# A graph network kernel: scatter one-hots of two layers read once for 13 of 25 tiles, those of the attention layer built during the propagation

## The reference

```python
h = relu(_layernorm(x)); x = x + propagate(h, src, dst)        # 10 iterations
#   msg = h[src] * norm[src];  agg = segment_sum(msg, dst)
#   h = 0.9 * agg * norm + 0.1 * h0
h = relu(_layernorm(x)); x = x + attention(h, rows=src, cols=dst, q, k, v)
#   att = exp(clip(q[rows] . k[cols])) per head, normalised over rows
#   out = segment_sum(att * v[cols], rows)
h = relu(_layernorm(x)); x = x + neighbours(h, edge_weight, ...)
#   segment_sum(h[src] * weight, dst) / deg, two 64x64 products
h = relu(_layernorm(x)); x = x + reviews(h * cj, ...) * ci
#   segment_sum(sigmoid(edge_attr @ ps_w) * h[src], dst)
```

## Time and profile before

| | |
|---|---|
| median of 3 runs | 1431.04 us (1430.93 to 1431.52) |
| profiled execution | 1421.67 us, its span 1420.0 us |
| TensorE matmuls busy | 1038.1 us (73%) |
| VectorE busy | 958.2 us (67%) |
| ScalarE busy | 566.7 us (40%) |
| GpSimd busy | 715.1 us (50%) |
| mean granted TensorE clock | 0.826 |
| DMA moved | 169.86 MB, mean 120 GB/s |

### The profile page before, as it was taken

One profiled execution on the slowest core, in us unless ns is written; L12 is line 12 of the kernel. 1 busy time (PEld: TensorE's weight loads), 2 busy tenths in 40 slices (PEclk: granted clock), 3 DMA queues, 4 the chain that ended last, 5 costly groups with the idle time before them and its releaser, 6 DMA issues.

```text
span 1420.0 us, 32164 instructions
## 1 busy us (share of the span) xinstructions
PE 1038.1 (73%) x12016; PEld 802.3 (57%) x12016; DVE 958.2 (67%) x1175; ACT 566.7 (40%) x1381; POOL 715.1 (50%) x444
## 2 busy tenths in 40 slices
PE   4956567877999999999934677767762766646764
PEld 3635457763555555555524677766662666545664
DVE  7885779993223223223255999999997788558875
ACT  1321127662010101101113766666651777417773
POOL 1000018888787878787888899999940000000000
PEclk9977655567999999999967878888765999759997
DMA  7642006551000000000012544444411889418894
GB/s 153 137 102 70 23 14 208 180 190 30 2 2 2 1 1 1 1 1 2 2 51 52 192 145 145 161 153 156 156 67 50 330 321 344 159 42 328 326 334 147
DMA packets 61492, 169.86 MB, mean 120 GB/s; under 512 B 32531, under 2 KB 33331, under 8 KB 61437
## 3 DMA queue, kind: packets, MB, share of 16 engines
q1 hardware_dynamic: 45371, 154.59, 30.5%
q10 hardware_dynamic: 2465, 13.60, 4.1%
q0 software_dynamic: 13600, 0.92, 3.5%
HBM read 144.28 MB, written 24.33 MB: 119 GB/s over the span
## 4 chain that ended last, share of the span: by engine, by line
PE 39%; DVE 31%; issue 15%; DMA 9%; ACT 3%; DVEq 2%; SPq 1%; ACTq 0%
PE ps L1424 24%; DMA hl_room<-slot_rows 7%; PE ps L1410 4%; DVE arena L809 3%; DVE base_room L804 3%; PE ps L1237 3%; PE ps L1298 2%; PE ps L1255 2%; DVE hl_room L998 2%; DMA hl_room<-in_edge_attr_dram 2%; DVE arena L886 2%; PE ps L1285 2%; DVE h_room L823 2%; DVE arena L823 1%; ACT arena L561 1%
## 5 line engine op out<-in xcount | busy, mean ns | idle before, releaser
L489 POOL DMA_INDIRECT w_table<-wpa,slot_i x425 | 710.4, 1672 | 329.3 <-ACT wpa L600 200.1
L1237 PE MATMUL ps<-arena 125*128 125x64 f16 (+1 forms) x3900 | 257.2, 218 | 165.7 <-ACT arena L528 75.6
L1424 PE MATMUL ps<-arena,hl_room 125*128 125x500 f16 (+1 forms) x1750 | 345.1, 353 | 9.1 <-DVEq L1062 9.1
L1237 PEld LDWEIGHTS ps<-arena 125*128 125x128 bf16 x3900 | 189.8, 105 | 181.8 <-ACT arena L528 74.6
L1424 PEld LDWEIGHTS ps<-arena,hl_room 125*128 125x128 f16 x1750 | 161.6, 100 | 169.7 <-issue 13.2
L1074 DVE TENSOR_TENSOR h_room<-ps,coef 125x256 f32<-125x256 f32 (+1 forms) x70 | 27.7, 396 | 271.5 <-PE ps L1410 271.5
L629 ACT ACTIVATE part_room<-ps 128x500 f32<-128x500 f32 (+1 forms) x70 | 38.0, 543 | 349.7 <-PE ps L1424 349.7
L1255 PE MATMUL ps<-arena 128*128 128x128 f16 (+1 forms) x1950 | 142.7, 238 | 21.6 <-DVE arena L818 9.8
L1242 PE MATMUL ps<-arena 125*128 (+1 forms) x1300 | 149.6, 214 | 0.0
L1255 PEld LDWEIGHTS ps<-arena 128*128 128x128 bf16 x1950 | 131.2, 108 | 24.3 <-issue 22.0
L791 DVE TENSOR_SCALAR arena<-hl_room,lane 125x3328 bf16<-125x3328 bf16 x100 | 108.3, 1086 | 48.8 <-DMA hl_room<-slot_rows 47.5
(11 more groups left out here) (244 smaller groups left out, 1336.1 us busy)
## 6 DMA issues: line engine op xcount, KB each, us to landing
hl_room<-slot_rows SPq DMA_DIRECT2D x100, 832.0 KB, 5.6
arena<-ohd_table SPq DMA_DIRECT2D x50, 832.0 KB, 5.8
hl_room<-in_edge_attr_dram ACTq DMA_DIRECT2D x17, 750.0 KB
w_table<-wpa,slot_i POOLq DMA_INDIRECT x425
ohd_table<-hl_room SPq DMA_DIRECT2D x13, 448.0 KB, 2.6
ohd_table<-base_room SPq DMA_DIRECT2D x12, 448.0 KB, 2.6
ohd_table<-hl_room SPq DMA_DIRECT2D x13, 384.0 KB
ohd_table<-base_room SPq DMA_DIRECT2D x12, 384.0 KB
```

The costliest lines, as they stand in the source:

```text
L489: pool.indirect_dma_start(w_table, bass.IndirectOffsetOnAxis(slot_i[:, u:u + 1], 0), wpa[:, u], None).then_inc(S[f"w_out{g % 2}"], 16)
L1237: last = pe.matmul(ps[:, m % RING, o:o + b - a], ohT[:, par, 0, k * L:(k + 1) * L], rhs, start=(i == 0), stop=(i == 1))
L1424: last = pe.matmul(ps[:, c, 0:w], hl[0:P, u, s, :], adj[:, s, c * CH * P:c * CH * P + w], start=(s == 0), stop=(s == T - 1))
```

## The change

1. **Layers 2 and 3:** the scatter one-hots of the even tiles (13 of 25) are loaded once, after the sums of the attention layer are taken, and stay in `kept_words` for both layers. Those of odd tiles are loaded in each layer into one room. TensorE waits for all kept loads before layer 2. The tables `parts2`, `ohT2` and `sums2` of these layers have places of their own.
2. **Attention layer:** VectorE no longer makes the scatter one-hots there. It makes them by halves during the propagation, after chunks 1 to 5 of each iteration, in the room of `xs`; SyncE writes each half to a table `ohs_table` in DRAM and loads a tile's one-hot (832 KB) in the layer. x is loaded again from the input after the last half is written, and VectorE waits for it before it goes on after the propagation.
3. **Propagation:** `part` is now a high and a low part in f16. ScalarE writes the high part scaled by 1/4096, VectorE the low part from PSUM and the high part; `combine` adds both with f16 matmuls, two per node tile, with 128 columns of weights instead of 125, and `coef` carries the factor. The bank of a chunk is free after VectorE's read.
4. **Edge weights:** the sigmoid is done in two parts: for 10 of 17 pieces of the features before the branch on the flag, for the other 7 in the old place. GpSimd starts its scatters after the first part and waits for the second before column 250. Its queue also issues the load of `wsl`, after the propagation.

```diff
                 def body(d, par, on, pair_no):
...
+                    if 2 in on and p == "l1":
+                        sp.wait_ge(S["l1_scat"], d - 1)
+                        sp.dma_start(ohd_words[:, par], ohs_table[bass.ds(d - 2, 1)].rearrange("t p x -> p (t x)")
+                                     ).then_inc(S[f"l1_ohd{par}"], 16)
+                    if 2 in on and p != "l1" and par:
                         sp.wait_ge(S[p + "_scat"], d - 1)
-                        sp.dma_start(ohd_words[:, par], ohd_table[bass.ds(d - 2, 1)].rearrange("t p x -> p (t x)")
-                                     ).then_inc(S[p + f"_ohd{par}"], 16)
+                        sp.dma_start(odd_words, ohd_table[bass.ds(d - 2, 1)].rearrange("t p x -> p (t x)")
+                                     ).then_inc(S[p + "_odd_oh"], 16)
...
+                with sp.Fori(0, T) as t:
+                    for half in range(2):
+                        a = sum(KG[:half]) * OW
+                        sp.wait_ge(S["ohs_made"], t * 2 + (half + 1))
+                        sp.dma_start(ohs_table[bass.ds(t, 1), :, a:a + KG[half] * OW].rearrange("t p x -> p (t x)"), ohs_words[half]
+                                     ).then_inc(S[f"ohs_out{half}"], 16)
+                for half in range(2):
+                    sp.wait_ge(S[f"ohs_out{half}"], 16 * (T + 1))
+                for a, b in SPLIT:
+                    sp.dma_start(xs[a:b, :, :], x.rearrange("(t p) f -> p t f", p=P)[a:b]).then_inc(S["x_back"], 16)
...
-                sp.wait_ge(S["w_placed"], 1)
-                sp.dma_start(wsl, w_table.rearrange("(r q) c -> r q c", r=L)).then_inc(S["wsl_in"], 16)
                 one_hots_kept(sp)
+                sp.wait_ge(S["l1_agg"], 1)
+                for k in range((T + 1) // 2):
+                    sp.dma_start(kept_words[:, k], ohd_table[2 * k]).then_inc(S["kept_in"], 16)
                 load_rows("l2", (0,))
...
                 for g in range(J // SU):
+                    if g * SU == EARLY * CJ:
+                        pool.wait_ge(S["pa_ready"], 2)
...
-                pool.sem_inc(S["w_placed"], 1)
+                pool.wait_ge(S["l0_done"], 1)
+                pool.dma_start(wsl, w_table.rearrange("(r q) c -> r q c", r=L)).then_inc(S["wsl_in"], 16)
...
             turned_features(0, EA_FLAG)
+            turned_logits(EARLY - 1)
+            act.wait_ge(S["z_back"], 1)
+            act.activation(wpa[:, 0:EARLY * CJ, 1], ps[0:P, 4, 0:EARLY * CJ], ACT.Sigmoid).then_inc(S["pa_ready"], 1)
...
-                            act.activation(part[:, n % 2, 0:w], ps[:, c, 0:w], ACT.Copy).then_inc(S["mains_taken"], 1)
+                            act.activation(part[:, n % 2, 0, 0:w], ps[:, c, 0:w], ACT.Copy, scale=1 / PSCALE).then_inc(S["part_high"], 1)
...
-                def ohd_of(s, par):
-
-                    vec.wait_ge(S[p + "_scat"], s - 1)
-                    vec.tensor_tensor(ohd[par], nodes(C), pairs(sls_h[:, bass.ds((s - 2) * C, C)], C),
-                                      ALU.is_equal).then_inc(S[p + "_ohd"], 1)
...
+                def low_sums(i, n):
+                    c = n % NCH
+                    w = min(CH, T - CH * c) * P
+                    vec.wait_ge(S["part_high"], i * (2 * NCH) + (n + 1))
+                    vec.scalar_tensor_tensor(part[:, n % 2, 1, 0:w], ps[:, c, 0:w], 1 / PSCALE, part[:, n % 2, 0, 0:w],
+                                             ALU.mult, ALU.subtract).then_inc(S["mains_taken"], 1)
...
+                def scatter_one_hots(t, k):
+                    j, half = k // 2, k % 2
+                    c, n = sum(KG[:half]), KG[half]
+                    vec.wait_ge(S[f"ohs_out{half}"], (t + j) * 16 + 16)
+                    vec.tensor_tensor(ohs_half[half], nodes(n), pairs(sls_h[:, bass.ds((t + j) * C + c, n)], n), ALU.is_equal
+                                      ).then_inc(S["ohs_made"], 1)
...
+                def two_iterations(i, more):
+                    for n in range(2 * NCH):
+                        u, c = n // NCH, n % NCH
+                        turn = c == NCH - 1
+                        if turn:
+                            new_nodes(i, n)
+                        if more or n + 1 < 2 * NCH:
+                            low_sums(i, n + 1)
+                        if not turn:
+                            new_nodes(i, n)
+                        if 1 <= c <= 5:
+                            scatter_one_hots(i * (T // (K0 // 2)), u * 5 + (c - 1))
...
                 vec.sem_inc(S["l0_done"], 1)
+                vec.wait_ge(S["x_back"], 32)
...
+                if p == "l2":
+                    pe.wait_ge(S["kept_in"], 16 * ((T + 1) // 2))
...
+                        if p == "l1":
+                            place = ohd[par][:, k // 2, :, k % 2]
+                        elif par:
+                            place = odd_oh[:, k // 2, :, k % 2]
+                        else:
+                            place = kept_oh[:, bass.ds(room, 1), k // 2, :, k % 2].rearrange("p k r -> p (k r)")
...
+            pe.wait_ge(S["z_turned"], EARLY)
+            for c in range(EARLY):
+                last = pe.transpose(ps[0:P, 4, c * CJ:(c + 1) * CJ], zT[0:CJ, c], ident[0:CJ, 0:CJ])
+            last.then_inc(S["z_back"], 1)
+            pe.wait_ge(S["pa_ready"], 1)
...
                     for k in range(min(CH, T - CH * c)):
-                        last = pe.matmul(ps[0:P, 7, k * D:(k + 1) * D], part[:, odd, k * P:(k + 1) * P], pair[:, :], start=True, stop=True)
+                        for e in range(2):
+                            last = pe.matmul(ps[:, 7, k * D:(k + 1) * D], part[:, odd, e, k * P:k * P + L], pair[:, :],
+                                             start=(e == 0), stop=(e == 1))
                     last.then_inc(S["combined"], 1)
```

149 lines of the change are left out of this document (85 added, 64 removed).

## The result

The changed kernel takes 1380.95 us (median of 4 runs, 1371.74 to 1385.22) beside 1431.28 for the kernel before in the same series: ratio 0.9634, 95% interval 0.9582 to 0.9685. The forecast was 1383, its range 1363 to 1408.

What follows compares the result with a forecast made beforehand. TensorE bounds the propagation, VectorE the attention layer, row loads layers 2 and 3. Terms -1.0 - 9.2 - 36 + 10 - 12 = -48.2 us take the profiled 1421.67 to 1373.5, median 1383; own range 1373 to 1394, wider 1363 to 1408.

Steps and rivals of the forecast that it cites:

- up to the propagation: Before the adjacency stage: transposes and a sigmoid moved early shorten VectorE's wait, 1.0 us off (0 to 1.5).
- propagation and reload, A to C: First multiplication of the propagation to the residual sum: combine gain less boundary waits, late end and reload, -9.2 us (-22 to +5).
- attention layer: Attention layer: tile period from 11.34 to 9.9 us, set by loads in SyncE's queue, 25 tiles: -36 us (-45 to -13).
- kept load, E to F: Attention sums to layer 2's first low part: 13 kept loads delay layer 2 by 10 us (6 to 14).
- layers 2 and 3: Layers 2 and 3: fewer one-hot loads, 4.8 us a tile, 6 us a layer, 12 us off in both (4 to 16).
- Combine: Propagation: f16 combine takes 0.27 us a chunk instead of 0.82, 32.8 us off in all (21 to 34).
- Boundary: Iteration ends in the propagation: TensorE waits 1.5 us for VectorE's updates, nine times, 13.5 us back (5 to 25).
- Rival (b): Propagation gives nothing back: each iteration boundary costs 3.5 us instead of 1.5, +18, time 1401; chance 0.14.
- Tail and reload: End of the propagation: last update ends later, +2.3 us, and VectorE waits for reloaded x, +7.8 (5 to 9).
- Rival (a): Attention layer held by loads: pair lands after 9 us, period 10.8, layer gives 13 us, time 1406; chance 0.17.
- (d): Slower through SyncE's queue: attention-layer loads land later than 11.0 us; at 12 us, period 12.3, time 1443; chance 0.04.
- Edge weights and the early sigmoid: GpSimd's scatters start about 110 us sooner, end near 950 to 990, before layer 2 wants the weights: hidden, 0.

Runs made afterwards that it cites:

- a1: The changed kernel once more, with no edit: 1373.66 us, ratio 0.9634 to the kernel before.
- c2: Changed kernel with VectorE building scatter one-hots in the attention layer again, none in the propagation, x not reloaded: 1380.64 us, ratio 0.9692.
- b2: a4 without the reload of x; the residual sum reads one-hots in its place, so part of the result is left out: 1366.68 us, ratio 0.9525.
- b4: a4 plus the edits of b1 and b3, and two kept tiles loaded ahead of the attention layer: 1361.68 us, ratio 0.9495.
- a4: Changed kernel with the attention layer's scatter one-hot loads issued by ScalarE instead of SyncE: 1359.35 us, ratio 0.9529.
- b3: a4 with the rows of layer 2's first two tiles loaded before the 13 kept loads, TensorE waiting at the first scatter: 1364.13 us, ratio 0.951.
- a2: Changed kernel with GpSimd's scatters starting only after the second sigmoid; early transposes and sigmoid stay: 1372.82 us, ratio 0.9624.
- a3: Changed kernel with the early part undone: all 17 transposes and one sigmoid behind the sort, GpSimd starting after them: 1377.61 us, ratio 0.9662.
- second series: Four edited kernels built on a4, b1 to b4, run on one chip beside the kernel before, whose median there was 1435.00 us.
- c4: a4 once more, with no edit, in the third series: 1359.74 us, ratio 0.9517.
- b1: a4 with the halves of scatter one-hots made in chunks 0 to 4 of each iteration instead of 1 to 5: 1365.49 us, ratio 0.9537.
- c1: a4 with VectorE's wait for the reloaded x moved behind the branch, directly ahead of the sum that needs it: 1356.39 us, ratio 0.9502.

## Why the prediction was right

Measured by a1 against the profile of before (the changed kernel's own profile in brackets), from the table. a1 is taken because its start of the propagation is that of the kernel before; the medians of the two series are 50.3 and 52.6 us apart.

| term | predicted | measured |
|---|---|---|
| up to the propagation | -1.0 | -0.6 (+10.1) |
| propagation and reload, A to C | -9.2 | -15.9 (-15.7) |
| C to D | 0 | +0.1 (-0.2) |
| attention layer | -36 | -26.2 (-25.7) |
| kept load, E to F | +10 | +7.1 (+6.9) |
| layers 2 and 3 | -12 | -13.5 (-11.9) |
| sum | -48.2 | -49.0 (-36.5) |

The mechanisms were right, stage by stage, but that the sum is right to 1 us is luck: an error of 10 us in the attention layer is cancelled by three of 1.5 to 6.7 on the other side.

**Combine.** 0.23 us instead of the 0.27 taken: 0.59 off a chunk, 35 us over the propagation by the prediction's own count (58 x 0.59 + 9 x 0.1). The nearest row, 33 ns a matmul, was the right one of the two; the measured 0.23 us is 29 ns each. (The other row gives 56 ns, 1.39 / 25, and not 59.)

**Boundary.** A to B fell by 27.0, so 8 of the 35 came back, not 13.5: 0.9 us an iteration instead of 1.5. c2 splits it: without the one-hots A to B falls by 32.6, so the one-hots cost 5.6 us, and 2.5 stay with the low sums and the shorter combine, which no run separates. The chain of VectorE's steps is the right mechanism, counted a little long: its last step ends 8.0 us after chunk 5's matmuls (449.5 to 457.5 in the timeline above), where 8.5 was worked out, and TensorE wants it at 7.7 (457.54 less the 0.35 of waiting), not 7.1. So the wait itself is a third of the 1.5, 0.48 us in the mean, less than the 1 to 2 us named as a sign. Most of the rest is in short waits of about 0.2 us ahead of the combine and of the next matmuls, 2.3 us in all, which c2 has too. Rival (b) is out.

**Tail and reload.** +10.1 predicted (2.3 and 7.8), +11.1 measured. Both transfers took longer than the sum had them: x is issued at 709.59 and awaited until 717.85, 8.3 us (6 taken), and in a1's chain the write takes 3.1 us (2.6 taken). So the wait was 10.72, but what the reload costs is 5.5 to 6.7 us (b2), since the gap behind the branch was shorter: 3.2 to 3.8 us in most kernels that wait there, 5.6 before and 5.95 in b2. That the wait shortens the gap is not shown: b4 has a wait of 9.5 and a gap of 6.0.

**Attention layer.** This is the term that was mis-sized most. The loop over SyncE's queue was named and a4 shows it: with the one-hots in another queue the period is 9.54, as VectorE alone would have it. But T was put at 9.9 for every tile; from the fifth pitch on it alternates between 9.55 and 10.8 or more, 10.15 in the mean of 24 pitches (766.6 to 1010.1 in a1). That is 6 of the 10 us. The loop closes over two tiles with the prediction's own three terms: the one-hot load is issued 6.06 us after the product (857.60 to 863.66), the rows are used 6.7 later (870.36), and the next but one product starts 7.74 after that (878.10), 20.5 us for two tiles. Two of the terms were right or long (7.74 and 7.06). The one that failed is the end of the scatter, put at 4.7 us with bounds of 3.4 to 5.3 (the row gives 3.5 for the lower): in the tile that sets the loop it is 6.06, in the other 3.93; why it ends so late there, no run isolates. The other 4 us are bookkeeping: I took 25 periods at 11.34, and the old layer has 24 pitches with a mean of 11.23 (782.4 to 1052.0) and a start and an end that do not shrink. (11.23 - 10.15) x 24 = 26. Rival (a), T 10.8 by a late landing, is out, since the pair lands within those 6.7 us; so is (d).

**Kept load.** 31.3 us from the sums to the first use of a row (34.3 predicted): 421 GB/s in the middle of it, where I had taken 370. The row of 418 GB/s was the better guide. The Trainium skill, page "DMA: Bandwidth & Descriptors", section Specifications, has about 358 GB/s as a core's HBM limit; the row there derives it as half of what two cores share. The trace, of a program on one core, does not stay under it: 421 GB/s for tiles that are read once each. The prediction said that layer 2 can start on nothing else because TensorE waits for all 13; the wait that the trace shows is VectorE's for the rows queued behind them (7.08 us), and TensorE's first matmul of the layer waits for the one-hot made from those rows. b3 moves both and takes 6 us of the late start back by order alone, for 1 us more later.

**Layers 2 and 3.** 4.82 and 4.80 us a tile in the mean of a1's two layers, where 4.8 was said, after 5.06 and 5.11: the loop of three engines (4.75) is the bound in most tiles. Some 6.5 us of waiting for rows are left in each layer.

**Edge weights and the early sigmoid.** Hidden, as said; the scatters end at 829, where 950 to 990 was said. They are hidden without the early start too: 976 to 986 at the latest (a2, a3). My reading that the old order leaves little carried the pace of the old attention layer over. There the scatters stood 4.2 us apart; in a3 they stand 2.7 apart, and in c2, which builds its one-hots in the attention layer as before, 3.6. In a4, whose VectorE has no gaps, they stand 2.9 apart, so it is not the lack of gaps alone that held them; what does, no run isolates.

**What stays open.** Why the profiled execution of the changed kernel lost 10 us ahead of the propagation, and why all four kernels of the second series started 11 to 15 us later there: not the edit (a1, a2, a3; c4 is b1's base and starts at 334.7). The second series ran on another chip, and its kernel before was 9 us slower than in the other two as well; whether the chip makes the difference is not tested. And what the gap behind the branch is made of: 0.60, 3.2 to 3.8 or 5.6 to 6.2 us at the same place in different kernels.

## What to carry to other kernels

When a load is put into a queue that also feeds the pacing engine, look at what it waits for: every load behind it inherits that wait. Here the queue of another engine, which made that wait anyway, gave back 14 us for one moved load (a4). Put a wait directly ahead of the instruction that needs it, behind branches and independent steps (c1: 4.5 us of the stage), and a bulk load behind the first loads of the stage that it serves (b3: 6 us of the late start). Before a stage difference between two profiles is explained, profile the same kernel twice.

## What had not been expected of the hardware

- An unedited kernel reached the same instruction at 332.8 and at 343.5 us in two executions of different series, with each later stage equal to 1.6 us.
- 13 loads of 832 KB, each read once, ran at 421 GB/s over 24 us with the DMA engines' share at 1.02 (a1: 421 over 20 us).
- The gap at the end of a branch varied from 0.60 to 6.24 us from kernel to kernel, and none showed when a wait for a load stood behind the branch (c1, the sum 4.5 us sooner).
- GpSimd's indirect scatters stood 4.2 us apart while VectorE built one-hots in the attention layer (before), and 2.4 to 2.9 where it did not (a1 to a4).
